# Moving the input-tile loads of a fused attention and ternary FFN kernel from SyncE's DMA queue to GpSimd's

## The chip, the cores and the metric

The kernel runs on all 8 cores of one Trainium2 chip. Each core takes 2 of the 16 sequences and does the same work with the same weights; the cores exchange nothing. The metric is the device time in microseconds of the slowest core.

## The reference

One transformer layer in two parts, on x of 16 x 2048 x 1024 in float32. (The code below is cut; `ln` is a layer norm without weights.)

```python
x = x + attn(ln(x))          # 16 heads of 64, causal window of 128 keys
x = x + ffn(ln(x))           # BitLinear 1024 -> 4096, gelu, BitLinear 4096 -> 1024

def attn(x):                 # qkv = x @ w_qkv ; softmax over allowed = (j <= i) & (j > i - 128)
    return softmax(q @ k.T / 8) @ v @ w_out

def bitlinear(x, W, b):
    w_scale = mean(abs(W));  Wq = clip(round(W / w_scale), -1, 1) * w_scale   # ternary weights
    x_scale = max(abs(x), axis=-1)
    xq = clip(round(x * 127 / x_scale), -128, 127) * x_scale / 127            # 8-bit activations
    return xq @ Wq.T + b
```

## The kernel before

A core has 4096 tokens, worked on as 32 tiles of 128 tokens (T = 128, nt = 32). Instructions are collected in one list by `op` and `dma` and written out per engine in that order, each with explicit semaphore waits. An engine works through its own list in order, so an instruction that waits holds up all behind it on that engine. The DMA issues of a queue are part of its engine's list: "syncq" is SyncE (SP), "pool" is GpSimd (POOL), "act" is ScalarE. POOL computes nothing here, it only issues DMAs.

**Start.** ScalarE's queue loads w_qkv and w_out, which VectorE and ScalarE cast to bf16 by turns. The loads of the first two input tiles (xin, two buffers) are issued at line 264.

**Attention loop**, t = 0 to 31, one tile each turn, software-pipelined by a tile. Turn t begins with `a_ln1_stats(t + 1)`: ScalarE squares the next input tile with an accumulator (L489) and VectorE reduces it to its sum (L493); the small operations L496, L500 and L503 on VectorE and L507 and L511 on ScalarE make mean and inverse deviation of it. Only behind these, in the order of both engines, come the row maxima (VectorE, L659 and L664) and the exponentials (ScalarE, L686) of the softmax of tile t. The heads go in four groups of scores, softmax, transposes (L737), copies (L748) and product with v (L766). In between, `a_ln1_apply(t + 1)` writes xln (L525), TensorE transposes it and computes q of the next tile (`a_qkv`, L559 into psA), k (into psB) and, at the end of the turn, v (into psC). Near the end `a_outproj(t)` (L790) and `a_res(t)` run: VectorE adds the input tile xin to the projection and writes x1buf (L801), and POOL's queue stores that to x1_d (the x1sp issue). Then TensorE does the v projection of tile t + 1 and VectorE casts it to v_hist (L583). After `a_ln2_acc(t)` comes the load of input tile t + 2 into the buffer that L801 has just finished reading (the issue is line 912, printed by its helper at L185). It waits for L801 and for L525 of tile t.

Between these steps 258 weight-preparation tasks are dripped in, some eight a turn: in the first half of the turns VectorE sums the absolute values of W1 and W2, in the second half it quantizes them (L421, L426, L430), TensorE transposes them (L443), and VectorE copies them to W1qT (L455) or to w2st (L464), from which SP's queue stores them to w2td. The weight pieces (wstage, four buffers) are loaded on SP's queue.

**Feed-forward loop**, 32 tiles, with the weights resident: x1 tiles are loaded on SP's queue, VectorE rounds, TensorE does both products, y is stored on POOL's queue. xin isn't used there.

Of the kernel before, what the change touches and what calls it, by code (L numbers as in the profile page):

```python
# [18 lines left out]
T = 128  # L19
# [24 lines left out]
def _build(nt, mode="full", cut=None):  # L44
# [3 lines left out]
    xc = nc.dram_tensor("xc", [ntok, D], F32, kind="ExternalInput").ap()  # L48
# [16 lines left out]
    def sb(name, p, n, dt, at=None):  # L65
        size = n * mybir.dt.size(dt)
        o = cur[0] if at is None else at
        o = (o + 31) & ~31
        h = nc._state.alloc_sbuf_tensor_at(name, [p, n], dt, offset=o)
        if at is None:  # L70
            cur[0] = o + size
        return h.ap()
# [32 lines left out]
    xin = [sb("xin0", 128, D, F32), sb("xin1", 128, D, F32)]  # L105
# [45 lines left out]
    with ExitStack() as ctx:  # L151
# [7 lines left out]
        dX = _Sem("dX"); dS = _Sem("dS"); dL = _Sem("dL"); dO = _Sem("dO")  # L159
# [11 lines left out]
        def op(ek, fn, waits=(), inc=None, amt=1, is_dma=False,  # L171
               nosync=False):
            if fn is not None and not is_dma and ek in _ES:
                inc = _ES[ek]
                amt = 1
            OPS.append((ek, [w for w in waits if w is not None and w[1] > 0],
                        fn, inc, amt, is_dma, nosync))
            if inc is not None:
                inc.n += amt
                return inc.n  # L180
            return None

        def dma(ek, out_ap, in_ap, sem, waits=()):
            w = [(sem, sem.n)] + list(waits)
            return op(ek, (lambda e, o=out_ap, i=in_ap: e.dma_start(out=o, in_=i)),  # L185
                      w, sem, 16, is_dma=True)
# [25 lines left out]
        def fence(gt):  # L212
            if gt < 2:
                return
            for ek in ("pe", "dve", "act", "pool"):
                waits = [(ENG_SEM[o], eng_end[o][gt - 1])
                         for o in ("pe", "dve", "act", "pool") if o != ek]
                op(ek, None, waits=waits)

        def tile_end():  # L220
            for ek in ("pe", "dve", "act", "pool"):
                eng_end[ek].append(ENG_SEM[ek].n)
# [38 lines left out]

        xin_ld = {}
        for t0 in range(min(2, nt)):
            xin_ld[t0] = dma("syncq", xin[t0 % 2], xc[t0 * T:(t0 + 1) * T, :], dX)

        wc_v, wc_a = 0, 0
        stg_rd = {0: None, 1: None}
# [218 lines left out]
        def a_ln1_stats(t):  # L486
            par = t % 2
            cl = cells[t % 2]
            va = op("act", lambda e, x=xin[par], c=cl: e.activation(  # L489
                out=outbuf, in_=x, func=AF.Square,  # L490
                accum_out=c[:, CEL_SSQ:CEL_SSQ + 1]),
                waits=[(dX, xin_ld[t])], inc=sA)
            op("dve", lambda e, x=xin[par], c=cl: e.tensor_reduce(  # L493
                out=c[:, CEL_SUM:CEL_SUM + 1], in_=x, axis=AX.X, op=ALU.add),
                waits=[(dX, xin_ld[t])], nosync=True)
            vm = op("dve", lambda e, c=cl: e.tensor_scalar(  # L496
                out=c[:, CEL_M:CEL_M + 1], in0=c[:, CEL_SUM:CEL_SUM + 1],
                scalar1=1.0 / D, scalar2=None, op0=ALU.mult), inc=sV)
            ms[("ln1m", t)] = vm
            op("dve", lambda e, c=cl: e.tensor_tensor(  # L500
                out=c[:, CEL_MSQ:CEL_MSQ + 1], in0=c[:, CEL_M:CEL_M + 1],
                in1=c[:, CEL_M:CEL_M + 1], op=ALU.mult))
            v = op("dve", lambda e, c=cl: e.scalar_tensor_tensor(  # L503
                out=c[:, CEL_VAR:CEL_VAR + 1], in0=c[:, CEL_SSQ:CEL_SSQ + 1],
                scalar=1.0 / D, in1=c[:, CEL_MSQ:CEL_MSQ + 1],
                op0=ALU.mult, op1=ALU.subtract), waits=[(sA, va)], inc=sV)
            op("act", lambda e, c=cl: e.activation(  # L507
                out=c[:, CEL_LNV:CEL_LNV + 1], in_=c[:, CEL_VAR:CEL_VAR + 1],
                func=AF.Ln, bias=c_eps),
                waits=[(sV, v), (sV, ms["memset"])])  # L510
            va = op("act", lambda e, c=cl: e.activation(  # L511
                out=c[:, CEL_RSTD:CEL_RSTD + 1], in_=c[:, CEL_LNV:CEL_LNV + 1],
                func=AF.Exp, scale=-0.5), inc=sA)
            ms[("rstd", t)] = va
# [75 lines left out]
        def a_qkT(t):  # L590
            par = t % 2
            for src_name, buf, wkey in (("q", q_sb, ("q_sb", t)),
                                        ("k", k_sb, ("k_sb", t))):
                wsem = sA if src_name == "q" else sV
                for r in range(2):
                    sp, key = next_stage()
                    pv = None
                    for hh in range(8):
                        h = r * 8 + hh
                        pv = op("pe", lambda e, b=buf, h_=h, hh_=hh, p=sp:  # L600
                                e.transpose(
                            out=p[0:64, hh_ * 128:(hh_ + 1) * 128],
                            in_=b[:, h_ * 64:(h_ + 1) * 64], identity=identb),
                            waits=([(wsem, ms[wkey]), psum_free[key]]
                                   if hh == 0 else []),
                            inc=(sP if hh == 7 else None))
                    if src_name == "q":
                        dst = qT[0:64, r * 1024:(r + 1) * 1024]
                    else:
                        dst = kT_hist[0:64, par * 2048 + r * 1024:  # L610
                                      par * 2048 + (r + 1) * 1024]
                    v = op("act", lambda e, d=dst, p=sp: e.copy(  # L612
                        out=d, in_=p[0:64, 0:1024]),
                        waits=[(sP, pv), (sP, ms.get(("scores", t - 1, 3), 0))],
                        inc=sA, nosync=True)
                    psum_free[key] = (sA, v)
                ms[("qT", t) if src_name == "q" else ("kT", t)] = v
# [232 lines left out]
        for t in range(nt):  # L850
            fence(gtile)
            gtile += 1
            ptasks = list(prep_by_tile[t])

            def prep_drip(k):
                for _ in range(k):
                    if ptasks:
                        prep_emit(ptasks.pop(0))

            if t + 1 < nt:  # L860
                a_ln1_stats(t + 1)
            if t == 0:
                a_qkT(0)
            a_scores(t, 0)
            a_sm_max(t, 0)
            a_sm_exp(t, 0)
            if t > 0:
                a_ln2_fin(t - 1)
            a_scores(t, 1)
            a_sm_max(t, 1)  # L870
            a_sm_exp(t, 1)
            a_sm_norm(t, 0)
            a_scores(t, 2)
            a_sm_max(t, 2)
            prep_drip(2)
            a_pt(t, 0)
            a_av(t, 0)
            prep_flushT()
            a_sm_exp(t, 2)
            a_sm_norm(t, 1)  # L880
            if t + 1 < nt:
                a_ln1_apply(t + 1)
            a_scores(t, 3)
            a_sm_max(t, 3)
            prep_drip(2)
            a_pt(t, 1)
            a_av(t, 1)
            prep_flushT()
            a_sm_exp(t, 3)
            a_sm_norm(t, 2)  # L890
            if t + 1 < nt:
                a_xlnT(t + 1)
            prep_drip(2)
            a_pt(t, 2)
            a_av(t, 2)
            prep_flushT()
            if t + 1 < nt:
                a_qkv(t + 1, 0)
            a_sm_norm(t, 3)
            a_pt(t, 3)  # L900
            a_av(t, 3)
            prep_drip(2)
            if t + 1 < nt:
                a_qkv(t + 1, 1)
                a_qkT(t + 1)
            a_outproj(t)
            a_res(t)
            if t + 1 < nt:
                a_qkv(t + 1, 2)
            a_ln2_acc(t)  # L910
            if t + 2 < nt:
                xin_ld[t + 2] = dma(
                    "syncq", xin[t % 2], xc[(t + 2) * T:(t + 3) * T, :],
                    dX, waits=[(sV, ms[("res", t)]), (sA, ms[("xln", t)])])
            prep_drip(len(ptasks))
            prep_flushT()
            tile_end()
# [421 lines left out]
```

How the kernel before makes its waits and increments, by code:

```python
        def run(eng):  # L1265
            lastw = {}
            zi = 0
            for (k, waits, fn, inc, amt, is_dma, ns) in OPS:
                if k != ek:
                    continue
                for (s, val) in waits:
                    if val > 0 and lastw.get(s.name, 0) < val:
                        eng.wait_ge(s.h, val)
                        lastw[s.name] = val
                if fn is None:
                    continue
                if zs is not None and zi > 0 and not ns:
                    eng.wait_ge(zs.h, zi)
                inst = fn(eng)
                if zs is not None and not is_dma:
                    zi += 1
                if inc is not None:
                    inst.then_inc(inc.h, amt)
```

## Time and profile before

| | |
|---|---|
| two runs | 3082.79 and 3113.27 us, median 3098.03 |
| the profiled execution | 3080.93 us; spans of the cores 3067.1 to 3079.4 us |
| TensorE matmul busy | 2249.6 us, 73% of the span |
| VectorE busy | 1959.7 us, 64% |
| ScalarE busy | 1068.0 us, 35% |
| GpSimd busy | 49.4 us, 2% |
| mean granted TensorE clock | 0.857 to 0.859 on all cores |
| xin load, issue to landing | 4.6 us (median of 32) |
| x1sp store, issue to landing | 5.5 us (median of 32) |

One execution on the chip is recorded; the page and the views are of the slowest core (core 5), with times from the start of its span. An engine's idle time before an instruction is put down to what released it. PEclk is the TensorE clock granted, 1.00 being 2.4 GHz and 0.50 being 1.2 GHz. The attention loop takes the span up to about 1,670 us.

### The profile page before, as it was taken

How to read it: one execution, taken by the hardware profiler on the slowest of the kernel's cores; microseconds unless marked ns; L12 is line 12 of the kernel's file. 1: busy time of each engine (PE TensorE's matmuls, PEld its weight loads, DVE VectorE, ACT ScalarE, POOL GpSimd, SP SyncE). 2: the span in 40 equal slices, each digit the busy share in tenths (PEclk: the TensorE clock that was granted, in tenths of full speed). 3: DMA queues.
4: the chain of work that ended last, by engine and by line, in shares of the span. 5: the costliest groups of instructions: out<-in, count | busy, mean ns of one | idle time of the engine just before them, and what ended most of it. 6: DMA issues, size and time to landing. Idle time of an engine off the chain costs nothing.

```text
span 3079.4 us, 40322 instructions; the slowest of 8 cores (3067.1 to 3079.4 us)
## 1 busy us (share of the span) xinstructions
PE 2249.6 (73%) x13196; PEld 1083.7 (35%) x13196; DVE 1959.7 (64%) x3711; ACT 1068.0 (35%) x2064; POOL 49.4 (2%) x68
## 2 busy tenths in 40 slices
PE   0376777777767676767674888888888888888886
PEld 0133334333333333333332333333333333333332
DVE  1245545554556666666665777877778777787775
ACT  1245545554544444444442222222222222222221
POOL 0000000000000000000000000000000000000000
PEclk9977787778777777777776999999999999999998
DMA  4222222222212212223234100000000000000000
GB/s 153 96 72 83 67 71 69 83 62 76 66 59 66 62 63 62 73 80 85 81 85 125 64 28 14 28 28 28 27 15 28 28 28 28 15 28 28 28 21 14
DMA packets 94339, 170.65 MB, mean 55 GB/s; under 512 B 41138, under 2 KB 41394, under 8 KB 93619
## 3 DMA queue, kind: packets, MB, share of 16 engines
q1 hardware_dynamic: 79872, 109.08, 12.2%
q0 software_dynamic: 9216, 33.56, 2.7%
q10 hardware_dynamic: 5044, 25.44, 2.4%
q8 instruction: 108, 1.77, 0.3%
q14 instruction: 99, 0.81, 0.1%
HBM read 126.09 MB, written 41.95 MB: 55 GB/s over the span
## 4 chain that ended last, share of the span: by engine, by line
PE 60%; ACT 14%; DVE 11%; issue 7%; DMA 6%; ACTq 0%; DVEq 0%; SPq 0%; POOLq 0%
PE psC L1196 16%; PE psA L987 8%; PE psB L987 8%; PE psA L559 6%; ACT hqT L1179 4%; PE psC L790 4%; PE psB L559 4%; ACT probsT L748 3%; DMA xin<-xc 3%; DVE wqch L430 2%; ACT probs L686 2%; PE psC L559 2%; DMA wstgB<-wqkv 2%; ACT qT L612 1%; PE psA L979 1%
## 5 line engine op out<-in xcount | busy, mean ns | idle before, releaser
L1196 PE MATMUL psC<-W2qT,hqT 128*128 128x512 bf16 x2048 | 483.8, 388 | 121.5 <-ACT hqT L1179 121.5
L1196 PEld LDWEIGHTS psC<-W2qT,hqT 128*128 128x128 bf16 x2048 | 191.3, 99 | 364.7 <-issue 167.1
L1011 DVE TENSOR_REDUCE cells<-h_sb 128x1 f32<-128x1024 f32 x128 | 150.2, 1213 | 174.2 <-ACT h_sb L1004 174.2
L987 PE MATMUL psA<-W1qT,xqT 128*128 128x512 bf16 x1024 | 254.8, 394 | 0.0
L987 PE MATMUL psB<-W1qT,xqT 128*128 128x512 bf16 x1024 | 243.2, 380 | 0.0
L766 PE MATMUL psC<-probsT,v_hist 128*64 128x128 bf16 x1024 | 75.2, 289 | 181.1 <-ACT probsT L748 181.1
L959 DVE TENSOR_TENSOR tib<-t1a,tfb 128x1024 f32<-128x1024 f32 x160 | 196.1, 1225 | 17.0 <-DVE tfb L958 0.5
L577 DVE CAST k_sb<-psB 128x1024 bf16<-128x1024 f32 x32 | 39.2, 1224 | 250.0 <-PE psB L559 250.0
L559 PE MATMUL psA<-wqkv_sb,xlnT 128*128 128x512 bf16 x512 | 181.9, 533 | 1.4 <-ACT xlnT L543 1.4
L1179 ACT ACTIVATE hqT<-psF 128x1024 bf16<-128x1024 bf16 x64 | 65.5, 1024 | 325.8 <-PE psF L1169 325.8
L1179 ACT ACTIVATE hqT<-psD 128x1024 bf16<-128x1024 bf16 x64 | 65.5, 1024 | 323.7 <-PE psD L1169 323.7
L961 DVE SCALAR_TENSOR_TENSOR hq<-tfb,tib 128x1024 bf16<-128x1024 f32 x128 | 156.8, 1225 | 14.0 <-DVE tib L959 0.9
L559 PE MATMUL psC<-wqkv_sb,xlnT 128*128 128x512 bf16 x512 | 115.6, 379 | 47.8 <-DVE x1b L801 47.8
L634 PE MATMUL psA<-kT_hist,qT 64*128 64x128 bf16 x512 | 64.0, 262 | 117.0 <-ACT probs L686 115.8
L716 DVE TENSOR_SCALAR probs<-probs,cells 128x256 bf16<-128x256 bf16 x512 | 123.5, 283 | 38.0 <-DVE cells L703 23.3
L987 PEld LDWEIGHTS psA<-W1qT,xqT 128*128 128x128 bf16 x1024 | 91.8, 100 | 128.1 <-issue 42.4
L801 DVE TENSOR_TENSOR x1b<-psC,xin 128x1024 f32<-128x1024 f32 x32 | 39.2, 1224 | 149.2 <-PE psC L790 149.2
L987 PEld LDWEIGHTS psB<-W1qT,xqT 128*128 128x128 bf16 x1024 | 89.7, 98 | 119.7 <-issue 29.0
L766 PEld LDWEIGHTS psC<-probsT,v_hist 128*64 128x64 bf16 x1024 | 50.6, 146 | 208.5 <-issue 208.5
L686 ACT ACTIVATE probs<-psA,cells 128x256 bf16<-128x256 f32 x256 | 118.0, 473 | 12.2 <-DVE cells L659 6.2
L958 DVE CAST tfb<-tib 128x1024 f32<-128x1024 int32 x160 | 110.9, 693 | 17.5 <-DVE tib L957 1.4
L957 DVE CAST tib<-t1a 128x1024 int32<-128x1024 f32 x160 | 110.9, 693 | 17.2 <-DVE t1a L953 0.9
(160 smaller groups left out, 3764.1 us busy)
## 6 DMA issues: line engine op xcount, KB each, us to landing
wstage<-w SPq DMA_DIRECT2D x256, 256.0 KB, 2.8
xin<-xc SPq DMA_DIRECT2D x32, 512.0 KB, 4.6
x1sp<-x1b POOLq DMA_DIRECT2D x32, 512.0 KB, 5.5
y<-outbuf POOLq DMA_DIRECT2D x32, 512.0 KB, 4.3
x1b<-x1sp SPq DMA_DIRECT2D x22, 512.0 KB, 3.3
w2td<-w2st SPq DMA_DIRECT2D x64, 128.0 KB, 2.1
W2qT<-w2td ACTq DMA_DIRECT2D x4, 2048.0 KB, 13.7
wstgA<-wqkv ACTq DMA_DIRECT2D x8, 768.0 KB, 4.8
```

Source lines behind the costliest of these rows:

```text
L559: e.matmul(out=p[:, nn * 512:(nn + 1) * 512], lhsT=xlnT[:, cc * 128:(cc + 1) * 128], rhs=wqkv_sb[:, cc * 3 * D + g * D + nn * 512: cc * 3 ...
L686: e.activation(out=probs[g_ % 2][:, hh_ * 256:(hh_ + 1) * 256], in_=p[:, hh_ * 256:(hh_ + 1) * 256], func=AF.Exp, bias=c[:, CEL_NMX + 4 * ...
L716: v2 = op("dve", lambda e, c=cl, g_=g, hh_=hh: e.tensor_scalar(out=probsn[g_ % 2][:, hh_ * 256:(hh_ + 1) * 256], in0=probs[g_ % 2][:, hh_ ...
L766: kt_=kt, sl=slot, g_=g: e.matmul(out=psC[bp_:bp_ + 64, pp * 128:(pp + 1) * 128], lhsT=v_hist[:, sl * D + h_ * 64: sl * D + h_ * 64 + 64], ...
L790: pv = op("pe", lambda e, cc=c, nn=n: e.matmul(out=psC[:, nn * 512:(nn + 1) * 512], lhsT=attnout[:, cc * 128:(cc + 1) * 128], rhs=wout_sb[ ...
L957: op("dve", lambda e: e.tensor_copy(out=tib, in_=t1b))
L959: prev_cb = op("dve", lambda e: e.tensor_tensor(out=cbb, in0=t1b, in1=tfb, op=ALU.is_ge), inc=sV)
L961: rl = op("dve", lambda e, rr=r, d=dst_ap: e.scalar_tensor_tensor(out=d[:, rr * 1024:(rr + 1) * 1024], in0=tfb, scalar=-641.0, in1=cbb, op ...
L987: e.matmul(out=p[:, nn * 512:(nn + 1) * 512], lhsT=xqT[:, cc * 128:(cc + 1) * 128], rhs=W1qT[:, cc * HF + jj * 1024 + nn * 512: cc * HF + ...
L1011: op("dve", lambda e, jj=j, c=cl: e.tensor_reduce(out=c[:, FH + jj:FH + jj + 1], in_=h_sb[:, jj * 1024:(jj + 1) * 1024], axis=AX.X, op=ALU ...
L1179: evs = op("act", lambda e, rr_=rr, p=sp: e.activation(out=hqT[:, rr_ * 1024:(rr_ + 1) * 1024], in_=p, func=AF.Copy), waits=[(sP, pv)] + ( ...
L1196: pv = op("pe", lambda e, nn=n, kk=k: e.matmul(out=psC[:, nn * 512:(nn + 1) * 512], lhsT=hqT[:, kk * 128:(kk + 1) * 128], rhs=W2qT[:, kk * ...
```

## The change

Both loads of xin, the first two before the loop and the one at the end of each attention turn, are issued from POOL's queue ("pool") rather than from SP's ("syncq"). Size, addresses, semaphore (dX) and waits are unchanged. On POOL's queue, the load of turn t stands directly behind the x1sp store of turn t.

```diff
         xin_ld = {}
         for t0 in range(min(2, nt)):
-            xin_ld[t0] = dma("syncq", xin[t0 % 2], xc[t0 * T:(t0 + 1) * T, :], dX)
+            xin_ld[t0] = dma("pool", xin[t0 % 2], xc[t0 * T:(t0 + 1) * T, :], dX)
...
             if t + 2 < nt:
                 xin_ld[t + 2] = dma(
-                    "syncq", xin[t % 2], xc[(t + 2) * T:(t + 3) * T, :],
+                    "pool", xin[t % 2], xc[(t + 2) * T:(t + 3) * T, :],
                     dX, waits=[(sV, ms[("res", t)]), (sA, ms[("xln", t)])])
```

## Rows read from the trace of the kernel before

**Rows 1.** The page, part 2: granted TensorE clock in 40 equal slices

```profile
PEclk9977787778777777777776999999999999999998
```

**Rows 2.** The waits view: engine, line, what it waited for: us in total, times, longest

```profile
ACT outbuf L489 <- DMA xin<-xc: 74.3, 30, 4.0
...
DVE cells L493 <- DMA xin<-xc: 3.7, 5, 1.4
```

**Rows 3.** Timeline, usual tile, all engines: start, us, engine, line, operation [idle before]

```profile
583.82 1.23 DVE L801 TENSOR_TENSOR x1b<-psC,xin 128x1024 f32<-128x1024 f32 x1 [4.59 <-PE psC L790]
585.18 0.33 SPq L185 DMA_DIRECT2D xin<-xc  x1
...
585.58 0.53 POOL L185 DMA_DIRECT2D x1sp<-x1b  x1 [43.74 <-DVE x1b L801]
...
588.91 1.23 DVE L583 CAST v_hist<-psC 128x1024 bf16<-128x1024 f32 x1 [3.87 <-PE psC L559]
...
589.70 1.06 ACT L489 ACTIVATE outbuf<-xin 128x1024 f32<-128x1024 f32 x1 [2.12 <-DMA xin<-xc]
...
590.05 1.21 DVE L493 TENSOR_REDUCE cells<-xin 128x1 f32<-128x1024 f32 x1
```

**Rows 4.** Timeline, a tile that quantizes weights

```profile
1058.32 1.23 DVE L801 TENSOR_TENSOR x1b<-psC,xin 128x1024 f32<-128x1024 f32 x1 [4.59 <-PE psC L790]
...
1064.54 1.06 ACT L489 ACTIVATE outbuf<-xin 128x1024 f32<-128x1024 f32 x1 [2.46 <-DMA xin<-xc]
...
1065.22 1.21 DVE L493 TENSOR_REDUCE cells<-xin 128x1 f32<-128x1024 f32 x1
```

**Rows 5.** Timeline, the reduction in a tile whose load came late

```profile
280.82 1.22 DVE L493 TENSOR_REDUCE cells<-xin 128x1 f32<-128x1024 f32 x1 [1.43 <-DMA xin<-xc]
```

**Rows 6.** Busy time by stretch, usual tile; last three columns: PEclk, DMA share, GB/s

```profile
586.05:587.05 1.00, 1.00 (x6) 0.49 (x5) 0.00 (x0) 0.91 (x3) 0.06 (x1) 1.00 0.88 102
587.05:588.05 1.00, 1.00 (x7) 0.44 (x5) 0.00 (x0) 0.53 (x2) 0.00 (x0) 1.00 0.71 188
588.05:589.05 1.00, 1.00 (x8) 0.37 (x6) 0.14 (x1) 0.00 (x0) 0.00 (x0) 1.00 1.00 406
```

**Rows 7.** Busy time by stretch, after the add of the first tile without a load

```profile
1623.76:1624.76 1.00, 1.00 (x6) 0.49 (x5) 0.00 (x0) 0.91 (x3) 0.07 (x1) 1.00 0.42 168
1624.76:1625.76 1.00, 1.00 (x7) 0.44 (x5) 0.00 (x0) 0.54 (x2) 0.00 (x0) 1.00 0.92 360
```

**Rows 8.** Timeline of POOL, the store of that same tile

```profile
1623.30 0.53 POOL L185 DMA_DIRECT2D x1sp<-x1b  x1 [50.56 <-DVE x1b L801]
```

**Rows 9.** Busy time by stretch, from the start of the q projection; third from last: PEclk

```profile
299.85:302.92 3.07, 3.07 (x10) 1.14 (x9) 2.27 (x8) 0.00 (x0) 0.00 (x0) 0.50 0.58 166
...
609.15:613.53 4.38, 4.38 (x13) 1.62 (x12) 2.27 (x8) 0.00 (x0) 0.00 (x0) 0.50 0.57 170
613.53:615.00 1.47, 1.47 (x12) 0.74 (x11) 0.00 (x0) 0.00 (x0) 0.00 (x0) 1.00 0.37 134
...
884.92:886.60 1.68, 1.68 (x6) 0.61 (x5) 1.05 (x5) 0.00 (x0) 0.00 (x0) 0.50 0.37 141
```

**Rows 10.** Timeline of VectorE, residual adds L801 that end a tile

```profile
228.69 1.23 DVE L801 TENSOR_TENSOR x1b<-psC,xin 128x1024 f32<-128x1024 f32 x1 [4.53 <-PE psC L790]
273.08 1.23 DVE L801 TENSOR_TENSOR x1b<-psC,xin 128x1024 f32<-128x1024 f32 x1 [4.59 <-PE psC L790]
318.19 1.22 DVE L801 TENSOR_TENSOR x1b<-psC,xin 128x1024 f32<-128x1024 f32 x1 [4.59 <-PE psC L790]
362.02 1.23 DVE L801 TENSOR_TENSOR x1b<-psC,xin 128x1024 f32<-128x1024 f32 x1 [4.59 <-PE psC L790]
...
761.38 1.22 DVE L801 TENSOR_TENSOR x1b<-psC,xin 128x1024 f32<-128x1024 f32 x1 [4.59 <-PE psC L790]
...
1007.35 1.22 DVE L801 TENSOR_TENSOR x1b<-psC,xin 128x1024 f32<-128x1024 f32 x1 [4.59 <-PE psC L790]
...
1570.45 1.23 DVE L801 TENSOR_TENSOR x1b<-psC,xin 128x1024 f32<-128x1024 f32 x1 [4.60 <-PE psC L790]
```

## Prediction

> **What bounds the kernel now.** I read the page first: no engine is full over the span (TensorE leads, see the table above), and the PEclk line stays near 7 tenths until slice 24 and near 9 afterwards [rows 1]. So the span has two parts, the attention tiles and the feed-forward tiles. The changed load is used only in the first, which ends near 1,670 us, and I looked at nothing else closely.
>
> The waits view shows what the load costs today. ScalarE sat idle 74.3 us in all for xin, 30 times, and VectorE only 3.7 us, 5 times [rows 2]. The two numbers differ by twenty, and the timeline of one tile says why. Count from the end of the residual add L801 of a tile (585.05; I call it the mark). SP issues the load at +0.13, and POOL the store x1sp at +0.53. ScalarE starts its pass over the new tile (L489) at +4.65, after 2.12 us of idling. But VectorE is busy with the cast L583 until +5.09, and its own reduction of the same tile (L493) starts only then, with no idle time in front of it [rows 3]. The variance needs both passes, and VectorE's is the later one. In this tile the load has about 0.4 us of slack. In the tiles that quantize weights (from about 900 us on) VectorE also does the copies L455, and L493 starts 5.66 after its mark (1059.55), with the load in hand since about +4.99 [rows 4]: 0.7 to 1.0 us of slack. Only now and then is the load really late: in the tile with its mark at 274.31 it came at +6.5, and VectorE idled 1.43 us [rows 5]. So what ends last before the softmax of a tile is, nearly always, TensorE's v projection and the cast behind it, not the load.
>
> **The change part by part.** Nothing is added to or removed from the computation; 32 loads of 512 KB move from SP's queue to POOL's.
>
> *SP's queue.* It loses a load that waited for the residual add. What stands behind it are wstage loads and w2td stores, and each waits for VectorE's work that comes after that same add in VectorE's order. They can go no earlier than before: gain 0.
>
> *POOL's queue.* It holds one store per tile, and the load now stands right behind it. Its waits (the residual add, the xln pass long before, the previous xin) are met when the store goes. Behind the load is only the next tile's store, 44 us later. Nothing queues behind POOL: cost 0. The first two loads move too, but the first tile's reduction comes after all weight casts, at 118 us; the first load is hidden by over 100 us. I cost these at 0; without that cover they would cost a few us once.
>
> *The landing.* This is the term that matters. Now the store is issued after the load, and is slow to start because of it: in the us from +1 to +2 the 16 DMA engines are 0.88 busy for only 102 GB/s, 188 GB/s in the next, and 406 only in the fourth [rows 6]. The load's reads start slowly and the store's data come behind them. In the tile at 1622.76, the first that has no load left to issue, the store shows what it does alone: issued at +0.54 [rows 8], traffic 168 GB/s from +1 to +2 and 360 from +2 to +3 [rows 7], which is 528 KB in 2 us, so all of its 0.52 MB. The store is done at about +3.1 of its mark.
>
> After the change the store goes first, and the load's issue follows its 0.53 us record on POOL [rows 8], so at +1.07 instead of +0.13, 0.94 later. Bounds of the landing from the nearest rows:
> - low: the load's reads start under the store's writes, and it lands where it does now or slightly earlier, +4.65 [rows 3]. Then nothing moves.
> - high: it runs wholly behind the store. Now it takes 4.52 from issue to use, of which about 0.9 passes before traffic; 3.6 behind the store's end at +3.1 is +6.7, and with the spread of the late tiles (half a us in the mean, a tile like that of [rows 5] being 1.9 late) +7.2.
> - taken: issue at +1.07 plus the 4.52 of now is +5.6; the store keeps the 16 engines busy for 0.42 + 0.92 = 1.34 us [rows 7], of which I let somewhat under half fall on the load, giving +6.1. I take the middle, because reads that start slowly leave room for the writes, as [rows 6] show the other way round.
>
> The Trainium skill has a rule on this order: DMA: Bandwidth & Descriptors, section "Latency and other measured facts", gives about 1 us to the first byte from GpSimd and 0.6 from SP or ScalarE. By it alone the load would come 0.4 us later, +5.05, and the sum below would be nothing; my landing does not use it. The trace agrees with the 1 us only where no load runs beside the store.
>
> *What the landing costs.* At +6.1 the reduction L493 starts 1.1 later in the first kind of tile and 0.45 later in the quantizing tiles, about 15 loads each: 15 x 1.1 + 15 x 0.45 = 23 us if everything behind it moved one to one. It doesn't. The softmax chain moves, and the next tile's q projection (L559 into psA) with it; but this group runs its start at the lower clock. In the usual tile (start 609.15) 4.38 us of it pass at 0.5 before the clock rises; in the late tile (start 299.85) only 3.07 us do [rows 9]. The work is the same, so 1.31 us less at half clock gives back 0.65. And the next tile gives back more. The end marks [rows 10] make periods of 45.10 for the late tile (L801 ends 274.31 and 319.41) and 43.84 for the one behind it, against a mean of (761.38 - 228.69) / 12 = 44.39. Two tiles together took 88.94, against 88.78: a load 1.5 us late cost 0.2 us in the end. The trace shows a steady beat: full clock comes at 302.92 in the late tile and at 613.53 in the usual one, 7 periods later, 310.61 / 7 = 44.37 [rows 9]. While the clock rises on that beat, a tile that is later by d each time shortens the low-clock stretch by 2d, and its period stays. How far that goes is seen at 884.92, where only 1.68 us passed before the rise [rows 9]. From 4.4 down to 1.7 is 2.7, so a lasting lateness of up to 1.35 us costs nothing. The quantizing tiles beat at (1570.45 - 1007.35) / 11 = 51.19 [rows 10], and I carry the same room over to them; 0.45 is well inside. Without this cover the cost is the 23 us above.
>
> Both kinds are inside the room at +6.1, so the sum is 0 for the ordinary tiles. For the tiles with a straggling load, which now always meets the path, I add 5 us: one tile in four or so, 7 of 30, late by a further 1 us or so, most of the excess kept. The late tile of [rows 5] kept less; I stay on the cautious side.
>
> **Sum.** The profiled execution took 3080.9 us (3079.4 of span and 1.5 around it). 3080.9 + 5 = **3086 us**. The median of the two runs shown, 3098, lies 17 above the profiled one, and the two runs 30 apart, so anything within some 15 us of this says the same.
>
> **The rivals.**
> 1. *Wholly behind the store* (landing +7.2). For: one queue, and the store first. Against: the slow start of the load's reads is waiting, which can pass under writes. Reduction later by 2.2 and 1.55: 15 x 2.2 + 15 x 1.55 = 56 us one to one, less what the clock's beat takes, 0.85 and 0.2 beyond the room, 16 us at least: between 16 and 56, I say 34. Time 3115. Chance 22%.
> 2. *POOL's descriptor work is held up by VectorE* (the other side: slower by over 2%). The place is POOL's second record, from +1.07. If it can't go on while VectorE works, and ends only after the cast (+5.09), the load lands 3.4 after that, +8.5: later by 3.5 and 2.85, 95 us, 3176. It decides from a landing of about +8 on (3.0 and 2.35 later: 80 us one to one, 62 being 2%). Against it: VectorE is idle 3.87 us before the cast [rows 3], and 0.00 busy in the windows of [rows 7], so the record falls in a gap. The Trainium skill, SBUF — State Buffer, section "SBUF: two separate sides", states such a lock between VectorE's two-port modes and GpSimd's descriptor writes; the trace shows no case of it in this stretch, but every record of y in the feed-forward part is longer than those of x1sp, for a reason I don't know. Chance 6%.
> 3. *Faster, a little.* With the store out of the way early, and the load's reads close together, landing at or below +5.0 in every tile. That saves what VectorE waits now, 3.7 us [rows 2]: 3077. Chance 10%.
> 4. *My forecast*, hidden and absorbed: 62%.
>
> **How the numbers follow.** The likeliest is 3086, its own range 3072 to 3105. The range over all reaches up to rival 1 and the height of the second run: low 3070, high 3128; rival 2 and the far part of rival 1 stay out. A measurement of this kernel can tell about 2% from no change, 62 us. Slower by over that: rival 2 and a sliver of 1, 7%. Faster: nothing in the trace could give 62 us, 1%. Within: 92%.
>
> **What would show it.** In the profile after: POOL issues x1sp at +0.53 and xin near +1.1; ScalarE's L489 starts near +6.1 (right), +4.7 to +5.1 (rival 3), +7 (rival 1), +8 or more (rival 2). VectorE's idle time for xin before L493 rises from 3.7 to 15-30 us while the tile periods stay at 44.4 and 51.2 (right), or grow by more than half a us (wrong: no beat holds). The low-clock part of the q projection should shrink from 4.4 us to about 2 to 3. The store x1sp should land about 2 us sooner. Wrong for another reason would be a change in the feed-forward part, where nothing was touched.

## The result and the profile after

The changed kernel takes 3093.2 us (median of 9 runs, 3092.0 to 3095.7); the kernel before, run beside it, 3082.9. The ratio is 1.0037, with a 95% interval of 1.0025 to 1.0048: 10 us slower, well inside 2% and clear of the noise. The two runs of before that were shown ahead of the prediction had a median of 3098; the more numerous later ones lie at the level of its profiled execution, 3080.9. Some executions of most of these kernels take 20 to 120 us more, with the cores of one die at a lower granted clock than the other's; the ratios, and the medians of the experiments below, leave out those over about 1% longer.

The profiled execution after has a span of 3091.6 us (core 1 is the slowest). The waits view has the first difference, to be laid beside [rows 2]:

```profile
ACT outbuf L489 <- DMA xin<-xc: 115.7, 30, 5.1
...
DVE cells L493 <- DMA xin<-xc: 27.5, 29, 2.2
```

VectorE used to wait for the load 5 times, and now does so in 29 of 30 turns. The timeline of a usual turn, beside [rows 3] (columns as there; the mark, where L801 ends, is 635.99):

```profile
634.76 1.23 DVE L801 TENSOR_TENSOR x1b<-psC,xin 128x1024 f32<-128x1024 f32 x1 [4.59 <-PE psC L790]
...
636.54 0.54 POOL L185 DMA_DIRECT2D x1sp<-x1b  x1 [44.13 <-DVE x1b L801]
637.11 0.53 POOL L185 DMA_DIRECT2D xin<-xc  x1
639.85 1.23 DVE L583 CAST v_hist<-psC 128x1024 bf16<-128x1024 f32 x1 [3.87 <-PE psC L559]
642.25 1.22 DVE L493 TENSOR_REDUCE cells<-xin 128x1 f32<-128x1024 f32 x1 [1.17 <-DMA xin<-xc]
642.29 1.06 ACT L489 ACTIVATE outbuf<-xin 128x1024 f32<-128x1024 f32 x1 [3.76 <-DMA xin<-xc]
```

The load is issued at +1.12 and used at +6.30. Of the 1.4 us by which L489 is later here (over the 30 turns its median went from +4.87 to +6.3), 1.0 is the later issue (+1.12 against +0.13). The median start of L493 went from +5.0 to +6.3 in the first kind of turn and from +5.67 to +6.2 in the quantizing turns. Busy time by stretch in the same turn, beside [rows 6] (last columns: PEclk, DMA share, GB/s), shows the order of the transfers:

```profile
636.99:637.99 1.00, 1.00 (x6) 0.49 (x5) 0.00 (x0) 0.91 (x3) 0.61 (x2) 1.00 0.37 152
637.99:638.99 1.00, 1.00 (x7) 0.45 (x5) 0.00 (x0) 0.54 (x2) 0.00 (x0) 1.00 0.94 365
638.99:639.99 1.00, 1.00 (x8) 0.36 (x6) 0.14 (x1) 0.00 (x0) 0.00 (x0) 1.00 0.90 111
639.99:640.99 1.00, 1.00 (x11) 0.46 (x9) 1.00 (x1) 0.00 (x0) 0.00 (x0) 1.00 0.77 307
```

152 and 365 GB/s in the first two stretches are the store, as in [rows 7]; then come the load's reads, slow in their first us (0.90 busy for 111 GB/s) as they were before, and fast after. The store lands 3.0 us after its issue (median; 5.5 before), the load 5.1 (4.6 before).

So VectorE's reduction is late by 1.3 us in 15 turns and by 0.5 in 14 (medians). One to one that would be 26 us, and 10 were measured. Where the 10 came from is seen in the ends of the turns:

```profile
228.84 1.22 DVE L801 TENSOR_TENSOR x1b<-psC,xin 128x1024 f32<-128x1024 f32 x1 [4.53 <-PE psC L790]
273.41 1.22 DVE L801 TENSOR_TENSOR x1b<-psC,xin 128x1024 f32<-128x1024 f32 x1 [4.60 <-PE psC L790]
319.57 1.23 DVE L801 TENSOR_TENSOR x1b<-psC,xin 128x1024 f32<-128x1024 f32 x1 [4.60 <-PE psC L790]
364.65 1.23 DVE L801 TENSOR_TENSOR x1b<-psC,xin 128x1024 f32<-128x1024 f32 x1 [4.60 <-PE psC L790]
...
542.74 1.23 DVE L801 TENSOR_TENSOR x1b<-psC,xin 128x1024 f32<-128x1024 f32 x1 [4.59 <-PE psC L790]
589.54 1.23 DVE L801 TENSOR_TENSOR x1b<-psC,xin 128x1024 f32<-128x1024 f32 x1 [4.59 <-PE psC L790]
...
768.23 1.22 DVE L801 TENSOR_TENSOR x1b<-psC,xin 128x1024 f32<-128x1024 f32 x1 [4.59 <-PE psC L790]
...
1017.51 1.23 DVE L801 TENSOR_TENSOR x1b<-psC,xin 128x1024 f32<-128x1024 f32 x1 [4.60 <-PE psC L790]
...
1580.51 1.22 DVE L801 TENSOR_TENSOR x1b<-psC,xin 128x1024 f32<-128x1024 f32 x1 [4.59 <-PE psC L790]
```

Against [rows 10]: the quantizing turns keep their period, (1580.51 - 1017.51) / 11 = 51.18 against 51.19. The stretch between the two kinds of turn (768.23 to 1017.51) takes 249.28, against 1007.35 - 761.38 = 245.97: 3.3 more. The twelve turns from 228.84 to 768.23 take 539.39, against 532.69: 6.7 more. And of these most hold their 44.4; two do not, 46.17 (to 319.57) and 46.80 (to 589.54), each with a turn of about 45.1 behind it. 6.7 + 3.3 is the 10 us of the slowest core. The feed-forward part has no share that can be told: from the last L801 to the end of the span it takes 1414.8 us, against 1412.6 before, and it differs by 3 us and more between cores of one execution.

In both of those turns the clock rose late. Busy time by stretch, from the start of the q projection L559 to the rise, beside [rows 9] (third from last: PEclk); the first row is the turn before the first of the two, the fourth (570.30) is the second:

```profile
255.44:257.76 2.32, 2.32 (x8) 0.88 (x7) 2.00 (x7) 0.00 (x0) 0.00 (x0) 0.50 0.62 220
...
300.00:305.54 5.54, 5.54 (x16) 1.96 (x15) 2.27 (x8) 0.00 (x0) 0.00 (x0) 0.50 0.58 184
305.54:307.00 1.46, 1.26 (x12) 0.73 (x10) 0.00 (x0) 0.55 (x1) 0.00 (x0) 1.00 0.00 0
...
570.30:575.20 4.90, 4.90 (x14) 1.78 (x13) 2.26 (x8) 0.00 (x0) 0.00 (x0) 0.50 0.56 182
...
661.02:663.94 2.92, 2.92 (x9) 1.04 (x8) 2.27 (x8) 0.00 (x0) 0.00 (x0) 0.50 0.54 159
...
1101.05:1104.26 3.21, 3.21 (x10) 1.18 (x9) 2.51 (x10) 0.00 (x0) 0.00 (x0) 0.50 0.22 72
```

The usual turn now spends 2.92 us of the group at half clock instead of 4.38, the quantizing one 3.21. That is how they keep their period: in both kernels a turn ends 18.03 us plus half of this stretch after the group's start (661.02 + 18.03 + 1.46 = 680.51, which is the next mark; before, 609.15 + 18.03 + 2.19 = 629.37). In the turn from 274.63 the rise was due at 257.76 + 44.37 = 302.13, 2.13 after the group's start at 300.00. It came 3.4 us later, at 305.54, so that nearly the whole group ran at half clock (5.54 us). In the turn from 543.97 it was due 1.5 after the start and came 4.90 after it.

The other cores show the same. In the turn from 543.97 and the ones that match it on the other seven cores, the rise was due 1.1 to 1.9 us after the group's start, and on all eight it came 3.4 later. Four cores had one more late rise before, due 1.9 to 2.1 after the start. In the first half of the changed kernel no rise came in its place less than 2.0 us after the start, on any core.

### The profile page after: what moved, and what is told of

The parts are those of the page before. It is cut to its first block, busy times and chain, and to the rows that moved or that the text cites. A ratio compares the mean times of both kernels' runs of the same rounds, so it can differ in the third digit from the quotient of the medians.

```text
span 3091.6 us, 40292 instructions; the slowest of 8 cores (3077.1 to 3091.6 us)
## 1 busy us (share of the span) xinstructions
PE 2231.5 (72%) x13196; PEld 1078.1 (35%) x13196; DVE 1963.1 (63%) x3711; ACT 1069.8 (35%) x2064; POOL 66.5 (2%) x100
## 4 chain that ended last, share of the span: by engine, by line
PE 58%; ACT 13%; DVE 11%; DMA 8%; issue 8%; ACTq 0%; DVEq 0%; POOL 0%; POOLq 0%; SPq 0%
PE psC L1196 15%; PE psA L987 8%; PE psB L987 8%; PE psA L559 5%; DMA xin<-xc 5%; ACT hqT L1179 4%; PE psC L790 4%; PE psB L559 4%; ACT probsT L748 3%; DVE wqch L430 2%; ACT probs L686 2%; DMA wstgB<-wqkv 2%; ACT qT L612 1%; PE psA L979 1%; DVE sgnA L421 1%
## 5 line engine op out<-in xcount | busy, mean ns | idle before, releaser
L559 PE MATMUL psA<-wqkv_sb,xlnT 128*128 128x512 bf16 x512 | 164.4, 492 | 1.4 <-ACT xlnT L543 1.4
L559 PE MATMUL psC<-wqkv_sb,xlnT 128*128 128x512 bf16 x512 | 115.6, 379 | 47.8 <-DVE x1b L801 47.8
L801 DVE TENSOR_TENSOR x1b<-psC,xin 128x1024 f32<-128x1024 f32 x32 | 39.2, 1225 | 148.6 <-PE psC L790 148.6
```

The costliest lines, as they stand in the source:

```text
L559: e.matmul(out=p[:, nn * 512:(nn + 1) * 512], lhsT=xlnT[:, cc * 128:(cc + 1) * 128], rhs=wqkv_sb[:, cc * 3 * D + g * D + nn * 512: cc * 3 ...
```

## The experiments

Theory A: the load is late because on POOL's queue it stands behind the store. Theory D: what this costs is set by the granted clock, whose rise inside the q projection comes on a beat (the spacing of the rises is 44.4 us in the first half, 51.2 in the second); lateness shortens the half-clock stretch and costs nothing until a turn misses its place on the beat. Rivals: B, GpSimd as the issuer is the cause, whatever the order. C, lateness passes one to one. E, there is a fixed slack of another kind, and one to one beyond it.

The last column in the list below is the time from the first rise of the clock behind the first L801 to the last rise in the attention loop, mean of the 8 cores of the profiled execution, as difference from the kernel before (1450.7 us). It leaves the start and the feed-forward part out, which differ by a few us from core to core and execution to execution. "issue", "landing" and "L489" are medians of the slowest core: the load's issue after the mark, the time from issue to landing, and the start of L489 after the mark.

```
kernel              issue  landing  L489   ratio to before (95%)      loop
before              0.13    4.6     4.87
after               1.12    5.1     6.3    1.0037 (1.0025 to 1.0048)   +8.5
pool_load_first     0.62    4.8     5.57   1.0017 (1.0006 to 1.0027)   +1.2
sp_store_first      0.56    5.0     5.76   1.0001 (0.9990 to 1.0011)   +0.8
sp_load_plus1       1.38    4.2     5.7    1.0035 (1.0012 to 1.0057)   +5.9
sp_load_plus2       2.62    3.6     6.4    1.0056 (1.0040 to 1.0072)  +11.1
sp_load_plus5       5.17    3.8     9.08   1.0315 (1.0300 to 1.0331)  +95.1
three_buffers_sp    0.13    4.4     early  1.0031 (1.0003 to 1.0059)    0.0
three_buffers_pool  1.12    5.0     early  1.0024 (0.9992 to 1.0056)    0.0
stats_early         0.13    4.5     early  0.9740 (0.9704 to 0.9776)  -91.3
```

**Order and queue.** pool_load_first:

```diff
-            spill_ms[t] = dma("pool", x1_d[...], x1buf[par], dS, waits=[(sV, v)])
+            if t + 2 < nt:
+                xin_ld[t + 2] = dma("pool", xin[t % 2], xc[...], dX,
+                                    waits=[(sV, v), (sA, ms[("xln", t)])])
+            spill_ms[t] = dma("pool", x1_d[...], x1buf[par], dS, waits=[(sV, v)])
```

> Both xin loads stay on POOL's queue as in the changed kernel, but inside a turn the load is issued ahead of the x1sp store. Theory A (the load is late because it stands behind the store): ScalarE's L489 starts at +4.7 to +5.2 after the residual add, L493 follows the cast, full clock comes at 44.4 us spacing in every turn of the first half, and the time is that of the kernel before within 4 us. Rival B (the load is late because GpSimd issues it, whatever the order): L489 stays near +6.2 and the time near +10 us.

Measured: 3087.4 us, L489 at +5.57, no late rise on five of eight cores, one on each of the others. The timeline shows POOL's order turned round; the mark is 630.38:

```profile
631.00 0.53 POOL L185 DMA_DIRECT2D xin<-xc  x1 [43.33 <-DVE x1b L801]
631.52 0.54 POOL L185 DMA_DIRECT2D x1sp<-x1b  x1
...
635.58 1.22 DVE L493 TENSOR_REDUCE cells<-xin 128x1 f32<-128x1024 f32 x1
```

Half of the lateness is gone (1.4 to 0.7) and with it about half of the time and nearly all of the loop's difference. Neither A nor B alone: the order gives one half, 0.5 us of it because the load's issue no longer stands behind the store's record of 0.53 us, and 0.25 between issue and landing. The other half stays with POOL as the issuer: 0.5 of the 0.7 us is the later issue (+0.62 here, +0.13 from SP), 0.2 the way from issue to landing. The Trainium skill (DMA: Bandwidth & Descriptors, section "Latency and other measured facts") gives 1 us against 0.6 to the first byte, a difference of 0.4; the trace has a difference of the same sign, 0.2 from issue to landing (4.83 against 4.60) and 0.7 from the mark to the use of the data.

sp_store_first: the store goes to SP's queue, right ahead of the load.

```diff
-            spill_ms[t] = dma("pool", x1_d[...], x1buf[par], dS, waits=[(sV, v)])
+            spill_ms[t] = dma("syncq", x1_d[...], x1buf[par], dS, waits=[(sV, v)])
+            if t + 2 < nt:
+                xin_ld[t + 2] = dma("syncq", xin[t % 2], xc[...], dX, waits=[...])
```

> The load stays on SP's queue, and the x1sp store moves to SP's queue directly ahead of it; POOL issues only y. Theory A (order of store and load): the load is late here too, L489 at about +5.8 to +6.4, time 4 to 12 us above before. Rival B (GpSimd's queue itself): L489 at +4.7 to +5.0, the time of before.

Measured: 3081.4 us, L489 at +5.76 in the median, but between +4.7 and +6.6: in a third of the turns the load is about as early as before. So a store ahead of the load delays it on either queue (A; 0.4 us of it is the later issue, +0.56), but less surely than on POOL's, and the time doesn't move (my 4 to 12 us was a miss). Rises late: one on two cores, none on six.

**How much lateness costs.** The load stays on SP and waits for something later of the same turn: ScalarE's first pass over x1 (plus1), its second (plus2), or the cast L583 (plus5).

```diff
-                    dX, waits=[(sV, ms[("res", t)]), (sA, ms[("xln", t)])])
+                    dX, waits=[(sV, ms[("res", t)]), (sA, ms[("ln2s", t)])])    # plus1
+                    dX, waits=[(sV, ms[("res", t)]), (sA, ms[("ln2a", t)])])    # plus2
+                    dX, waits=[..., (sA, ms[("xln", t)]), (sV, ms[("v_sb", t + 1)])])  # plus5
```

> Queues as in the kernel before, but the load of turn t waits for ScalarE's first pass L813 over the new x1 tile, so it is issued near +1.3 instead of +0.13, about where POOL issues it after the change. Theory A: the store on POOL is then in front in time, L489 starts at +5.8 to +6.4, the time rises by 3 to 14 us, as with the change, without POOL issuing the load. Rival C (lateness passes one to one from the first 0.4 us on): with +6.1 it would be 15 x 1.1 + 15 x 0.45 = 23 us or more.

Measured: 3090.2 us, with L489 at +5.7 and L493 at +5.8 in the first half and on time in the second. The load on SP's queue, issued at +1.38, a little later than POOL issues it (+1.12), costs nearly as much as the change: POOL isn't needed for it.

> As the last, but the load waits for ScalarE's second pass L817 and goes near +2.6; L489 should start near +6.9 to +7.1. Theory D (the clock's beat takes up lateness only up to some 1.3 us; beyond it single turns get a full clock 3.4 us later): several turns of the first half at 47.8 instead of 44.4, and the time 30 to 50 us above before, all of it in whole steps of that size. Rival C (one to one, no room): 15 x 2.0 + 15 x 1.35 = 50 us, spread evenly over the turns. Rival E (a fixed slack of 0.6 us, beyond which it is one to one): 15 x 1.4 + 15 x 0.75 = 32 us, evenly.

Measured: 3098.8 us, 16 above before (0.40 to 0.72%), less than C's 50 and my own 30 to 50, because the load, issued when most of the store's traffic is over, needs only 3.6 us to land and L489 is at +6.4, not +7.0. At that lateness (medians of 1.55 in the first half, 0.6 in the second) C would give 15 x 1.55 + 14 x 0.6 = 32, which is out, and E 15 x 0.95 = 14, which is not. On the slowest core three of the first fourteen turns take 46.2 to 46.3 us and the others 44.5 to 45.6; the eight cores have between two and four late rises, counting the change from one kind of turn to the other. The quantizing turns keep 51.2.

> Queues as before, but the load of turn t waits for the cast L583 and is issued near +5.2; by the last run's 3.8 from issue to use, L489 should start near +9.0 to +9.4. Theory D (clock's beat, whole steps of 3.4 us): the first-half turns would go mostly 47.8 and 51.2, the second-half turns 54.6; time 85 to 110 us above before. Rival E (fixed slack of 0.6, one to one beyond): 15 x 3.6 + 15 x 2.9 = 98 us, evenly. The totals don't tell them apart, the list of turn periods does.

Measured: 3179.3 us, 97 above, as D and E both had it. The turns say more than the total. VectorE's adds that bound three neighbouring ones:

```profile
418.63 1.22 DVE L801 TENSOR_TENSOR x1b<-psC,xin 128x1024 f32<-128x1024 f32 x1 [4.59 <-PE psC L790]
466.41 1.22 DVE L801 TENSOR_TENSOR x1b<-psC,xin 128x1024 f32<-128x1024 f32 x1 [4.60 <-PE psC L790]
514.12 1.23 DVE L801 TENSOR_TENSOR x1b<-psC,xin 128x1024 f32<-128x1024 f32 x1 [4.59 <-PE psC L790]
562.11 1.22 DVE L801 TENSOR_TENSOR x1b<-psC,xin 128x1024 f32<-128x1024 f32 x1 [4.59 <-PE psC L790]
```

(562.11 - 418.63) / 3 = 47.8. All fourteen first-half turns of this core lie between 47.5 and 48.0 (D had expected some at 51.2 as well, and none came), and the spacing of the rises is 47.8 in every one of them on all cores. In sum over these fourteen turns L493 is later by 47 to 53 us on the eight cores and the turns are longer by 47 to 49. E, which takes off 0.6 us a turn, would give 39 to 44 and is too low; C fits these turns, but not those of the changed kernel and of sp_load_plus2. The quantizing turns separate them less well. On the slowest core L493 is 3.6 us later than before there and the turns, 54.65 in the mean, are 3.46 longer; over all cores it is 3.2 to 3.6 later and the turns 2.8 to 3.5 longer, where E has 2.6 to 3.0. At 0.5 us of lateness (the changed kernel) they were hardly longer, by 0.07 at most, which C does not allow.

**A load with a turn of cover.** A third xin buffer (two wstage buffers instead of four make room) lets each load go a turn earlier, on SP's or on POOL's queue.

```diff
-            if t + 2 < nt:
-                xin_ld[t + 2] = dma("syncq", xin[t % 2], xc[(t + 2) * T:(t + 3) * T, :], ...
+            if t + 3 < nt:
+                xin_ld[t + 3] = dma("syncq", xin[t % 3], xc[(t + 3) * T:(t + 4) * T, :], ...
```

> A third xin buffer (room from halving the wstage buffers to two) lets each load go a whole turn earlier, on SP's queue. Theory A: ScalarE and VectorE never wait for xin any more, L493 follows the cast in every turn, all first-half turns stay on the 44.4 beat, time 0 to 5 us under before (the 3.7 us that VectorE waits now are the most that can go). If two wstage buffers are too few, VectorE would wait for wstage loads, and the time would rise.

> The same with the loads on POOL's queue behind the store. Theory A: with a turn of cover the queue makes no difference, the time is that of three_buffers_sp within 3 us. Rival B (POOL as the issuer has a cost of its own, by descriptor work or shared rings): 4 us or more above three_buffers_sp.

Measured: 3083.8 and 3087.1 us in the median, 1.0031 and 1.0024, their intervals overlapping each other; five of the nine times of three_buffers_sp lie at 3080 to 3084 and four at 3099 to 3108, so these two can't be told apart by time, and the small gain that I had allowed for isn't there. In both traces ScalarE starts L489 at +2.63 in nearly every turn, and VectorE doesn't wait for xin at all:

```profile
582.52 1.23 DVE L801 TENSOR_TENSOR x1b<-psC,xin 128x1024 f32<-128x1024 f32 x1 [4.59 <-PE psC L790]
...
587.61 1.22 DVE L583 CAST v_hist<-psC 128x1024 bf16<-128x1024 f32 x1 [3.87 <-PE psC L559]
588.75 1.21 DVE L493 TENSOR_REDUCE cells<-xin 128x1 f32<-128x1024 f32 x1
```

The list of rises is the same in the two kernels, and the same as before the change on all but one core: the loop takes 1450.7 us in all three. So the few late loads of the kernel before cost nothing, and with cover the queue costs nothing in the loop. What remains open is why the feed-forward part took 5 us more in three_buffers_pool (1418.8 in the mean, from the last rise on) than in the others (1412 to 1417); nothing of it was changed.

**The start.** In spite of its label this kernel has only the two loads ahead of the loop on POOL's queue.

```diff
-            xin_ld[t0] = dma("syncq", xin[t0 % 2], xc[t0 * T:(t0 + 1) * T, :], dX)
+            xin_ld[t0] = dma("pool", xin[t0 % 2], xc[t0 * T:(t0 + 1) * T, :], dZ)
```

> Only the first two loads (before the loop) go to POOL's queue, with a semaphore of their own; the loop's loads stay on SP's. I costed this part at 0: time of the kernel before within 3 us. If the start or the feed-forward part carried some of the 10 us, it would show here.

Measured: 3082.9 us, 0.9997 (0.9972 to 1.0022), the loop 1450.7 in the mean. That part costs nothing.

**Taking the clock out.** Matmuls whose result is overwritten unused go into TensorE's idle stretches, in the kernel before and in the changed one.

```diff
+        def fill(k, c0, n):
+            for _ in range(k):
+                op("pe", lambda e, c=c0, m=n: e.matmul(out=psC[:, c:c + m], lhsT=identb,
+                    rhs=wqkv_sb[:, 0:m], start=True, stop=True), waits=[psum_free["C"]])
...
             a_scores(t, 1)
+            fill(14, 0, 512)
...
             a_pt(t, 0)
+            fill(10, 768, 256)
             a_av(t, 0)
```

> The kernel before, with matmuls whose result is overwritten unused placed in TensorE's idle stretches of each attention turn (14 of 128x512 after the scores of group 1, 10 of 128x256 between transposes and value product of groups 0 to 2, 4 after the scores of groups 2 and 3), so that the granted clock need not fall. If it stays at 1.00, the turns leave the 44.4 and 51.2 beat and are several us shorter (the half-clock share of the q projection alone gives 2.2 us, 65 us in all). If it falls anyway, the time stays within 30 us of before or rises.

Measured: 3000.8 us, 0.972 (0.968 to 0.977), 81 us faster than before. The clock line of its page, and then that of warm_after:

```profile
PEclk9999999999989999999997999999999999999998
```

```profile
PEclk9999999999989999999997999999999999998798
```

Against [rows 1] the sevens of the attention loop are gone, and in the first half so is the beat: over the first fourteen turns the clock is at half for 3 to 10 us of 577 to 580, where before it was for 283 to 287 of 620. In the quantizing turns it still falls in each, but briefly (55 to 68 us of 629 in thirteen turns; before, 348 to 355 of 665). The Trainium skill (TensorE: Matmul & The Clock Gate, section "What's actually happening") says that the low clock is the resting state and activity releases it; this trace agrees, with a mean granted clock of 0.962 to 0.964 on the cores against 0.857 to 0.859, the matmuls added being of no use to the result. They also change what TensorE has to do in these stretches, so what counts for theory D is the comparison of the two kernels that both have them. The first-half turns take 40.9 us when the load is in time. One that isn't can be seen at 433.18 (mark):

```profile
308.81 1.22 DVE L801 TENSOR_TENSOR x1b<-psC,xin 128x1024 f32<-128x1024 f32 x1 [4.59 <-PE psC L790]
349.70 1.22 DVE L801 TENSOR_TENSOR x1b<-psC,xin 128x1024 f32<-128x1024 f32 x1 [4.59 <-PE psC L790]
...
431.95 1.23 DVE L801 TENSOR_TENSOR x1b<-psC,xin 128x1024 f32<-128x1024 f32 x1 [4.59 <-PE psC L790]
439.64 1.22 DVE L493 TENSOR_REDUCE cells<-xin 128x1 f32<-128x1024 f32 x1 [1.37 <-DMA xin<-xc]
474.50 1.23 DVE L801 TENSOR_TENSOR x1b<-psC,xin 128x1024 f32<-128x1024 f32 x1 [4.59 <-PE psC L790]
```

L493 is at +6.46, 1.45 late, and the turn takes 42.55, 1.66 more than the 40.89 of the turn from 308.81. Nothing comes back in the next one (41.43, itself 0.5 late).

> The changed kernel (loads on POOL's queue) with the same additional matmuls. Theory D (it is the clock's rise that takes up the lateness): without a fall and rise the lateness of 1.25 and 0.55 us passes one to one, this is 15 x 1.25 + 14 x 0.55 = 26 us (20 to 32) slower than warm_before. Rival E (slack of another kind, in the engines' own order): it stays 10 us or less slower, as without them.

Measured: 3038.4 us, 38 above warm_before. The profiled execution is the slowest of four (3051.0; the others 3035.4 to 3038.4), so its parts have to be taken one by one. The first and last L801 of warm_before and then of warm_after, both on core 6:

```profile
184.93 1.22 DVE L801 TENSOR_TENSOR x1b<-psC,xin 128x1024 f32<-128x1024 f32 x1 [4.53 <-PE psC L790]
...
1586.85 1.22 DVE L801 TENSOR_TENSOR x1b<-psC,xin 128x1024 f32<-128x1024 f32 x1 [5.40 <-PE psC L790]
```

```profile
181.99 1.23 DVE L801 TENSOR_TENSOR x1b<-psC,xin 128x1024 f32<-128x1024 f32 x1 [4.53 <-PE psC L790]
...
1610.00 1.23 DVE L801 TENSOR_TENSOR x1b<-psC,xin 128x1024 f32<-128x1024 f32 x1 [6.29 <-PE psC L790]
```

The loop takes 1428.0 us against 1401.9, 26.1 more. On cores 2 to 7 it is 18 to 30 more, 26 in the mean, which is what theory D asks. In the first fourteen turns it is one to one on each of these six cores:

| core | L493 later, sum of 14 turns | turns longer, sum |
|---|---|---|
| 2 | 12.8 us | 12.9 us |
| 3 | 12.8 | 12.0 |
| 4 | 11.0 | 11.2 |
| 5 | 13.4 | 14.2 |
| 6 | 11.7 | 11.7 |
| 7 | 13.7 | 13.4 |

In the changed kernel without the added matmuls the same fourteen turns have L493 later by 11 to 16 us and are longer by only 4 to 8. In the thirteen quantizing turns of warm_after L493 is later by 8 to 10 us and the turns are longer by 8 to 14, a little more than one to one, where without the added matmuls they were hardly longer.

Two things in this execution don't belong to the load. On cores 0 and 1, whose loop is 48 and 51 us longer, the granted clock was 0.79 from 412 to 559 us; and on cores 2 and 3 it was about 0.8 in a stretch of the feed-forward part, where xin isn't loaded any more. Busy time of core 2, the slowest, in that stretch, first in warm_after and then in warm_before:

```profile
2753.80:2913.40 159.60, 136.35 (x567) 54.15 (x576) 110.42 (x160) 31.06 (x35) 3.05 (x3) 0.79 0.06 20
```

```profile
2753.80:2913.40 159.60, 133.47 (x659) 57.23 (x673) 123.54 (x178) 36.37 (x41) 4.08 (x4) 0.98 0.07 24
```

TensorE got through 567 matmuls there instead of 659, and the feed-forward part of that core takes 1435 us instead of 1408. Of the profiles kept only this one has such a stretch, and why is open. The three other executions weren't profiled; the mean span of their cores is 31 to 34 us above that of warm_before, and what they have beyond the 26 is open too.

**A version that beats both.** The wait for xin hides that VectorE idles 3.87 us between L801 and the cast. With three buffers the statistics of tile t + 2 fit there.

```diff
-            if t + 1 < nt:
-                a_ln1_stats(t + 1)
...
             a_res(t)
+            if t + 2 < nt:
+                a_ln1_stats(t + 2)
```

> three_buffers_sp, and the statistics of input tile t + 2 are placed right behind the residual add of turn t, where VectorE idles 3.87 us before the cast and ScalarE idles too. The row maxima then follow the cast (or the copies) directly, 1.85 us earlier in each turn. Rival E (one to one): 30 x 1.85 = 55 us less than before. Theory D (beat): the first half goes from 44.4 to 41.0 a turn, whole steps, 15 x 3.4 = 51 us; the second half wants 1.85 and gets it in a mixture of 51.2 and 47.8, some 28 us: 60 to 95 us less, 2990 to 3022.

Measured: 2998.4 us, 0.974 (0.970 to 0.978). The row maxima L659 follow the cast directly:

```profile
554.80 1.23 DVE L801 TENSOR_TENSOR x1b<-psC,xin 128x1024 f32<-128x1024 f32 x1 [4.59 <-PE psC L790]
555.94 1.21 DVE L493 TENSOR_REDUCE cells<-xin 128x1 f32<-128x1024 f32 x1
559.89 1.22 DVE L583 CAST v_hist<-psC 128x1024 bf16<-128x1024 f32 x1 [1.95 <-PE psC L559]
561.03 0.68 DVE L659 TENSOR_REDUCE cells<-psA 128x2 f32<-128x512 f32 x1
```

The chain is 1.9 us shorter a turn, 55 us one to one; the loop lost 91, since the rises went to a spacing of 41.0 in the first half and of 47.8 in the second, 3.4 less in each. For the second half I had expected a mixture, and it went down whole. No slack of another kind gives back more than was taken out of the chain.

> stats_early (three xin buffers, statistics placed in VectorE's idle stretch behind the residual add) with the additional matmuls of warm_before. If warm_before is faster than before by g, this should be faster than stats_early (2998) by about g as well, since one shortens the chain and the other the clock's low stretch.

Measured: 0.963 (0.958 to 0.968), 2972.5 to 2975.9 us, and a profiled span of 2974.2. The gains don't add up (some 25 more than stats_early, not 81, so the expectation was a miss). A likely reason, not tested by itself, is that stats_early has already taken about half of the half-clock stretch: 1.8 to 2.9 us of the group are left in most of its first-half turns and 1.4 to 2.3 in its quantizing ones.

## Why the prediction was partly right and wrong in its number

- **What bounds, and the slack.** Right. L493 behind the cast was the later of the two passes, and 0.4 and 0.7 us of slack were what the load had.
- **SP's and POOL's queues, the start: 0.** Right; loop_only_start_sp shows the start by itself.
- **The landing, +6.1.** Near: +6.3. The issue came at +1.12 (said: +1.07), the store landed 2.5 us sooner (said: 2). The bound below, that the load could land as early as before, was too generous; pool_load_first shows 0.7 us with POOL as the issuer even with nothing ahead.
- **The clock's beat.** Right as a mechanism: the half-clock stretch went from 4.4 to 2.9 us and most turns kept 44.4, all quantizing ones 51.2. warm_before and warm_after show it by its absence: there the lateness passes one to one in the first half, and costs 26 us in the loop (mean of six cores) instead of 10.
- **The term that failed** is the last one of the sum: "For the tiles with a straggling load [...] I add 5 us", and under it "a lasting lateness of up to 1.35 us costs nothing". The 5 us were 7 loads of 30, each late by a further 1 us. The trace of the slowest core has two such loads (L493 at +7.29 in the turn from 543.97, and at +7.57 in the turn from 1581.73, a quantizing one, where it cost nothing); what was lost came in three late rises of 3.3 us each, 10 and not 5, and only one of the three belongs to a straggler. The room of 1.35 was read at 884.92, in the turn where the kind of task changes. In the turns before it is smaller: with 2.0 us as the least stretch before a rise in its place, it is (4.4 - 2.0) / 2 = 1.2, less than the ordinary lateness of 1.3. So the turn from 274.63 missed its place with L493 at +6.32, within 0.1 us of its neighbours. Such a miss lengthens the stretches again (5.54 us, then 4.12, 3.40, 2.92), which is why it happens only now and then. The second miss is the straggler's, and that turn missed on all eight cores, with L493 between +6.8 and +7.5. The third is the change of tasks itself, near 840 to 915, where the shortest stretch of [rows 9] stood: two spacings of the rises make 109.2 us there, and 105.8 before. Four cores have only two late rises (+6.8 us in the loop), four have three (+10.2), the slowest among them.
- **The forecast's sign.** The sum was made against the profiled 3080.9, so 3086 meant 5 us slower; beside the median of 3098 it read as a gain of 12. The runs of before settled at 3082.9, and the change was a loss of 10.3 where the sum had 5. With two runs 30 us apart, I should have said which of the two levels I held for the kernel's.
- **The rivals.** Landing at +7.2 and more as a rule, or the load held up by VectorE's work, didn't happen: POOL's two records lie 0.03 us apart in VectorE's idle stretch. (That every record of y is longer than those of x1sp was misread: the medians are 1.02 and 0.53 us, but the shortest of y is 0.53 too.) Nor did rival 3, a small gain: its landing at or below +5.0 was never reached, and the 3.7 us of waiting that it would have saved cost nothing to begin with (three_buffers_sp).

## What to carry to other kernels

Where the granted clock falls and rises once in every turn of a loop, the turn's period can stick to the spacing of the rises: in these kernels a change of 1 or 2 us in the chain then cost or gained 0 or 3.4 in a turn, and a rival for small delays is "how much of the half-clock stretch is left". Read from the trace how long the engine runs at half clock before each rise and how near the shortest one is to the least ever seen, in turns of the same kind and on all cores; what a change uses up of that is no longer there for the late turns. And a load that waits for a buffer freed in the same turn wants to be first on its queue, or to have a third buffer. Before explaining a difference between two profiles, look for stretches where one core's granted clock is neither of its usual two levels, as in warm_after.

## What the runs showed that I had not expected

- Idle TensorE is dear here beyond its idle time: matmuls without use, 52 a turn, made the kernel 81 us faster (0.972), the mean granted clock going from 0.86 to 0.96.
- A load issued ahead of the store on POOL's queue still arrives 0.7 us later than from SP's (+5.57 against +4.87), 0.5 of it through the issue.
- The same 512 KB load from SP takes 3.6 us from issue to landing when it is issued 2.1 us after the store (sp_load_plus2), and 4.6 when it is issued 0.4 ahead of it (before).
- Shortening the chain by 1.9 us a turn gained 3.0 a turn (91 us over 30), as the beat moved down a step in both halves.
